# Layer 2's attention units in four steps instead of eight, and the places of three other groups of stages

## The chip, the core and the metric

The kernel runs on one core of a Trainium2 chip. The metric is the device time of one execution in microseconds. Before the change it is 1865.47 us, the median of three runs (1865.31 to 1870.87). One more execution was taken with the hardware profiler on: 1867.64 us, with a span of 1865.7 us from its first to its last instruction.

## What is computed

Four decoder-like layers run one after the other on x, 16 x 64 rows of 512 numbers. Each layer adds an attention over a context of the same shape and then a feed-forward part ("ffn"), and a layer norm stands before each of the eight. The code counts from zero (l0, f0, l1, f1 ...); this text says layer 1 for l0 and f0, layer 2 for l1 and f1, layer 3 for l2 and f2.

```python
x = x + L0_xattn(layernorm(x), ctx)   # layer 1: 8 heads, window of 16
x = x + L0_ffn(layernorm(x))          # int8-like quantised silu gate
x = x + L1_xattn(layernorm(x), ctx)   # layer 2: 32 query heads of 128, 8 key heads, RMS norm on q and k
x = x + L1_ffn(layernorm(x))          # one 512x512 product of MXFP4-quantised x and weight
x = x + L2_xattn(layernorm(x), ctx)   # layer 3: 32 heads of 16, 8 key heads
x = x + L2_ffn(layernorm(x))          # top 16 of 64 experts of rank 16
x = x + L3_xattn(layernorm(x), ctx)
x = x + L3_ffn(layernorm(x))
```

In layer 2's attention q and k of each head are divided by their root mean square, the scores go through a softmax, and the weighed values of four query heads go through a slice of the output matrix that is added to x. Its products are made three times (high times high, high times low, low times high part), for precision.

## The kernel before, in words

x lies in SBUF as eight tiles of 128 rows (NT = 8, two sequences each). The work is cut into stages, named by layer and part, and each stage has an index. A stage is a function on each of the engines that take part in it (TensorE, VectorE, ScalarE, GpSimd, SyncE for loads). `stage_order()` writes one list of (stage, index), ORDER, and every engine runs its own part of each stage in exactly that order; what crosses engines is held by semaphores. So the list sets each engine's queue. An instruction that waits holds everything behind it on its engine.

The list is made by pipelines. `pipeline(starts, stages, first)` gives, step by step, stage k of the unit that started k steps ago, latest stage first, but the stages named in `first` ahead of all. `beside(main, side, at)` makes one step of a main pipeline with two steps of a side pipeline: one ahead of it and one behind its first `at` stages.

- Layer 1's attention has 32 units (tile, quarter) of eight stages, one a step, 39 steps. Its ffn tiles are the side, one tile every eight side steps, that is every four main steps, with 13 stages (the last three make the layer norm and the transpose of layer 2). `at` is 4: in a step the order is side, l0_sum, l0_out, l0_weigh, l0_turn, side, l0_scores, l0_project, l0_rows, l0_norm.
- Layer 2's attention has 64 units (key head h, tile t; i = 8h + t) of eight stages: l1_a (12 query matmuls of 512 columns into bank 0 and 24 key and value matmuls of 256 into bank 1), l1_n (VectorE scales q and k by the reciprocal root mean square, which ScalarE's squares and GpSimd's power make), l1_b (transposes), l1_s (scores, row maximum, exps), l1_z (reciprocal, GpSimd's product), l1_t (probabilities turned), l1_v (weighing), l1_d (12 output matmuls and the addition to x). The order in a step is n, d, v, t, z, s, b, a. For the last head the copies of l1_b are ScalarE's, otherwise VectorE's.
- At the last tile of a head, ScalarE and VectorE split the next head's weights into high and low parts (`high_parts`, `low_parts`). At units 20, 24, 28 and 32 l1_d first quantises a tile of the ffn's weight (`mxfp4`, 11 VectorE instructions).
- The ffn tiles of layer 2 start with the last eight units. Each has eight stages: f1_stats, f1_norm, f1_quant (mxfp4), f1_turn, f1_mm, then l2_stats, l2_rows, l2_turn. f1_turn, f1_mm and l2_turn all use PSUM bank 3, which l1_b's keys also use.
- Behind the 71 steps `l2_begin` makes layer 3's keys and values in four groups of 12 matmuls, all four in bank 3. Then layer 3's attention starts (l2_q, l2_a, l2_s, l2_z, l2_t ...).

PSUM has eight banks. `psum_uses` gives each stage's banks; where a stage has several, they are taken in turn. A use waits until the last one of its bank is freed. In layer 1 the pair (6, 7) serves l0_out, the queries and keys of l0_project, and all the stages of the ffn with l1_turn.

Lines of the profile that the text speaks of: L557 a transpose of integers (f0_turn, f0_turn2), L564 a bf16 transpose (f1_turn), L608 layer 1's scores, L645 l0_out, L606 the band in front of the scores, L591 l0_project, L688 and L700 the queries and keys of l1_a, L712 l1_b, L724 l1_s, L732 l1_t, L739 l1_v, L749 l1_d; on VectorE L1157 the addition of l0_out, L1185 the silu's reciprocal, L1193 its end, L1047 a layer norm's rows, L1229 l1_n, L1086 the first of mxfp4, L1026 a layer norm's statistics; on GpSimd L1907 the power, L1882 the silu's product, L1849 the masked queries of l0_project; on ScalarE L1607 the keys' copy in l1_b.

Of the kernel before, what the change touches and what calls it, by code (L numbers as in the profile page):

```python
# [9 lines left out]
BF16 = mybir.dt.bfloat16  # L10
# [7 lines left out]
NT = 8  # L18
# [42 lines left out]
def stage_order():  # L61
    order = []
# [13 lines left out]
    def beside(main, side, at):  # L76

        run(1, side)
        got = next(main, [])
        order.extend(got[:at])  # L80
        run(1, side)
        order.extend(got[at:])
# [8 lines left out]
    l0 = ["l0_norm", "l0_rows", "l0_project", "l0_scores", "l0_sum", "l0_turn", "l0_weigh", "l0_out"]  # L91
# [34 lines left out]
    order.append(("f2_begin", 0))  # L126
    run(16 + 6 - 4, pipe2)
# [5 lines left out]
    for _ in range(10):  # L133
        beside(att3, ffn3, 3)
# [10 lines left out]
def psum_uses(stage, i):  # L145
# [15 lines left out]
    if stage in ("f0_gate", "f0_turn2", "f0_down", "l1_turn"):  # L161
        return [("p", (6, 7))]
    if stage == "l1_a":
        return [("q", (0,)), ("k", (1,))]
# [8 lines left out]
    if stage == "l2_begin":  # L173
        return [(k, (3,)) for k in range(4)]
# [108 lines left out]
def build_program(nc, d, out):  # L283
    ctx = ExitStack()
    with ctx:
# [137 lines left out]
        al = carve(R0, RF)  # L423
        CPt, CP = slots(al, 2, 528), slots(al, 3, 512)
# [4 lines left out]
        wq0, wk0, wv0 = al(128), al(128), al(128)  # L429
        wo0 = al(8 * 128).rearrange("p (h n) -> p h n", h=8)  # L430
        wob = CXf[0][:, 64:192]
        bq0, bk0, bo0 = al(1), al(1), al(1)
        bv0, hm = al(1), al(8)
        pad, band, bandb = al(384), al(640), al(640, BF16)
# [96 lines left out]
        def lt_user(kind, t):  # L531

            return {"l1": None, "l2": ("l1_a", 56 + t, "k"), "f2": ("l2_q", t // 2, 3), "l3": ("f2_h", t, 1),
                    "f3": ("l3_q", 24 + t // 4 * 4, 3)}[kind]


        def tensor_program(pe):
# [141 lines left out]
            def l1_a(i):  # L679
# [1546 lines left out]
```

## Time and profile before

| | |
|---|---|
| median of three runs | 1865.47 us |
| profiled execution | 1867.64 us, span 1865.7 us |
| TensorE matmuls busy | 1717.2 us, 92% |
| VectorE, ScalarE, GpSimd busy | 871.2, 712.5, 515.7 us |
| mean granted TensorE clock | 0.959 |
| DMA | 54.01 MB, mean 29 GB/s |

The granted clock is a share of full speed: 1 is 2.4 GHz, 0.5 is 1.2 GHz, and a stretch's value is the mean over both. The page cuts the span into 40 slices; each digit is the busy share of one in tenths:

```profile
PE   7999999689999999999999965699999998999997
PEclk9999889899999999999999987799999999999999
```

A row of the timeline gives start, duration, engine, line, operation, what it writes and reads and how many were merged; in brackets the idle time of the engine just before it and who ended it. Matmuls overlap, so the time that one takes from its engine is the distance to the next start, and not its duration.

### The profile page before, as it was taken

The numbers are of one execution on the slowest core, as the hardware profiler recorded it, in microseconds if no ns is written. First come the engines' busy times: TensorE is split into PE (matmuls) and PEld (weight loads), VectorE is DVE, ScalarE is ACT, GpSimd is POOL, SyncE is SP. The second block draws the span as 40 slices with busy tenths as digits, with TensorE's granted clock in tenths as the row PEclk, the third lists the DMA queues.
The fourth block names the chain that finished last, engine by engine and source line by source line (L and its number), as shares of the span: only waits on it lengthen the run. The fifth ranks groups of instructions, "written<-read, shape, count | busy, mean of one in ns | idle before, by whom it ended". The sixth has DMA issues, their size and how long they took to land. (4 is left out here: it accounts for less than half of the span.)

```text
span 1865.7 us, 26016 instructions
## 1 busy us (share of the span) xinstructions
PE 1717.2 (92%) x9694; PEld 1390.1 (75%) x9698; DVE 871.2 (47%) x1772; ACT 712.5 (38%) x2384; POOL 515.7 (28%) x615
## 2 busy tenths in 40 slices
PE   7999999689999999999999965699999998999997
PEld 5877787578888888888888853466555676777775
DVE  3566566444343445443433356567653321243344
ACT  3443333335454544444545531133221112354441
POOL 5566554222222221222222222233210000421122
PEclk9999889899999999999999987799999999999999
DMA  7000000111010000010101000020000012010000
GB/s 213 13 6 7 7 1 1 57 51 35 5 53 24 35 24 35 22 36 1 57 18 40 7 1 1 23 93 35 1 1 18 1 40 71 18 40 23 1 12 34
DMA packets 25709, 54.01 MB, mean 29 GB/s; under 512 B 14944, under 2 KB 16352, under 8 KB 22128
## 3 DMA queue, kind: packets, MB, share of 16 engines
q1 hardware_dynamic: 24048, 51.85, 8.3%
q8 instruction: 77, 1.26, 0.3%
q10 hardware_dynamic: 1472, 0.51, 0.1%
q14 instruction: 48, 0.39, 0.1%
q0 software_dynamic: 64, 0.00, 0.0%
HBM read 50.25 MB, written 2.10 MB: 28 GB/s over the span
## 5 line engine op out<-in xcount | busy, mean ns | idle before, releaser
L1912 POOL TENSOR_TENSOR big<-big 128x512 f32<-128x512 f32 x96 | 101.1, 1053 | 417.4 <-DVE big L1262 416.5
L1229 DVE TENSOR_TENSOR big<-pb,big 128x512 f32<-128x512 f32 x64 | 44.2, 691 | 362.3 <-POOL big L1907 362.3
L1617 ACT ACTIVATE big<-pb,big 128x128 f32<-128x128 f32 x384 | 135.7, 366 | 186.9 <-issue 113.7
L749 PE MATMUL pb<-woh,oh 128*128 128x512 f32 (+1 forms) x384 | 157.6, 411 | 2.5 <-DVE ol L1268 0.5
L1051 DVE TENSOR_TENSOR X<-X,pb 128x512 f32<-128x512 f32 x128 | 87.2, 681 | 148.1 <-PE pb L749 87.7
L1586 ACT ACTIVATE big<-pb 128x128 f32<-128x128 f32 x384 | 106.7, 278 | 123.6 <-PE pb L688 58.3
L749 PE MATMUL pb<-wol,oh 128*128 128x512 f32 (+1 forms) x384 | 153.5, 400 | 0.0
L749 PE MATMUL pb<-woh,ol 128*128 128x512 f32 (+1 forms) x384 | 153.1, 399 | 0.0
L700 PE MATMUL pb<-wkl,CXh 128*128 128x256 f32 x512 | 144.3, 282 | 0.0
L700 PE MATMUL pb<-wkh,CXh 128*128 128x256 f32 x512 | 144.1, 282 | 0.0
L700 PE MATMUL pb<-wkh,CXl 128*128 128x256 f32 x512 | 143.9, 281 | 0.0
L1633 ACT CAST oh<-pb 128x512 fp32r<-128x512 f32 (+1 forms) x96 | 56.0, 584 | 200.2 <-PE pb L739 199.9
L688 PE MATMUL pb<-wqh,CXh 128*128 128x512 f32 x256 | 110.0, 430 | 23.9 <-DVE big L1229 22.9
L1902 POOL TENSOR_SCALAR big<-big 128x6 f32<-128x6 f32 x64 | 12.8, 199 | 371.9 <-ACT big L1586 371.9
L688 PE MATMUL pb<-wqh,CXl 128*128 128x512 f32 x256 | 104.3, 407 | 0.0
L688 PE MATMUL pb<-wql,CXh 128*128 128x512 f32 x256 | 104.1, 407 | 0.0
L739 PE MATMUL pb<-big 128*128 128x256 f32 (+1 forms) x384 | 99.4, 381 | 0.0
L700 PEld LDWEIGHTS pb<-wkh,CXh 128*128 128x128 f32 x512 | 96.9, 189 | 3.0
L700 PEld LDWEIGHTS pb<-wkl,CXh 128*128 128x128 f32 x512 | 96.7, 189 | 3.0
L700 PEld LDWEIGHTS pb<-wkh,CXl 128*128 128x128 f32 x512 | 97.0, 190 | 0.0
L749 PEld LDWEIGHTS pb<-woh,oh 128*128 128x128 f32 (+1 forms) x384 | 74.7, 194 | 19.5 <-DVE ol L1268 6.1
L1907 POOL TENSOR_TENSOR big<-big,half 128x6 f32<-128x6 f32 x64 | 84.8, 1324 | 9.4
(246 smaller groups left out, 4066.8 us busy)
## 6 DMA issues: line engine op xcount, KB each, us to landing
big<-in_w SPq DMA_DIRECT2D x21, 1024.0 KB, 5.0
big<-in_w SPq DMA_DIRECT2D x8, 512.0 KB, 5.4
big<-in_w SPq DMA_DIRECT2D x4, 768.0 KB, 4.2
X<-in_x SPq DMA_DIRECT2D x8, 256.0 KB, 6.0
big<-in_cn SPq DMA_DIRECT2D x8, 256.0 KB, 2.7
CXlf<-in_cT SPq DMA_DIRECT2D x8, 256.0 KB, 5.3
big<-in_wa SPq DMA_DIRECT2D x1, 2048.0 KB, 7.6
big<-in_wb SPq DMA_DIRECT2D x1, 2048.0 KB, 12.0
```

Of the source, the lines that this page charges most:

```text
L688: a = pe.matmul(bank(p), x_rows(x, c, t), y[:, 512 * c:512 * c + 512], start=(n == 0), stop=(n == 11))
L700: a = pe.matmul(bank(p)[:, s * 256:s * 256 + 256], kv_rows(x, c, 2 * t + s), y[:, 256 * c:256 * c + 256], start=(n == 0), stop=(n == 11), ...
L739: a = pe.matmul(bank(p)[0:hd, s * 256:s * 256 + 256], v_of(s), pt[:, s * 256:s * 256 + 256], start=(s == 0), stop=True, skip_group_check=True)
L749: a = pe.matmul(bank(p), x[0:hd, 512 * k + h * 128:512 * k + h * 128 + 128], y[0:hd, 512 * h:512 * h + 512], start=(n == 0), stop=(n == 11))
L1051: v.tensor_tensor(X[:, t, :], X[:, t, :], bank(p), ADD).then_inc(p.free, 1)
L1229: v.tensor_tensor(quarters(qn[i % 2]), quarters(bank(p)), bc(rr[i % 2][:, 0:4], 128), MUL).then_inc(p.free, 1)
L1586: y = a.activation(sq[i % 2], src, ACT.Square, accum_out=ss[i % 2][:, j:j + 1])
L1617: y = a.activation(e_[:, c], bank(p)[:, c], ACT.Exp, bias=m[j % 2][:, k:k + 1], scale=1.0, accum_out=z[j % 2][:, k:k + 1])
L1633: a.copy(high[0:hd, k:k + 512].rearrange("p (h b q) -> p b h q", h=4, b=2), bank(p)[0:hd].rearrange("p (b h q) -> p b h q", b=2, h=4)).the ...
L1902: g.tensor_scalar(ss[i % 2][:, 0:6], ss[i % 2][:, 0:6], 1.0 / 128, 1e-6, MUL, ADD).then_inc(*on.to(S.pool))
L1907: g.tensor_tensor(rr[i % 2][:, 0:6], ss[i % 2][:, 0:6], half[:, 0:6], ALU.pow).then_inc(*on.to(S.rr))
L1912: g.tensor_tensor(quarters(e_), quarters(e_), bc(r[j % 2], 128), MUL).then_inc(*on.to(S.pn))
```

## The change

`beside` goes. `together(stages, *sides)` puts side steps at chosen places between the stages of one step, and `unit_steps` gives the stages of a step from a list with a delay for each, in the order in which the list has them.

- Layer 1: the same delays and nearly the same order, but the two side steps stand at places 2 and 5: l0_sum, l0_out, side, l0_weigh, l0_turn, l0_scores, side, l0_project, l0_rows, l0_norm. l1_turn uses bank 3 (with l0_turn) instead of the pair (6, 7). `l1_begin` stands three steps earlier; ScalarE waits there for layer 1's last scores and no longer for its last output, and buffers are laid out so that the two don't overlap.
- Layer 2: l1_a becomes l1_q and l1_k. The delays are 0 for q, k, n; 1 for b, s, z; 2 for t, v; 3 for d. The order in a step is q, b, t, k, s, n, z, v, d. 67 steps instead of 71. ScalarE squares q and then splits the next query weights, squares k, copies v and then splits the key weights; VectorE's low parts of the key weights come behind l1_n. The first output weights are split at unit 2 (was 1), and mxfp4 stands behind the addition.
- The ffn of layer 2 has its side steps at places 3 and 6 of the steps 60 to 65, both behind the output in step 66, and the last eight in layer 3's first steps.
- Layer 3's keys: the four groups of `l2_begin` become the stage `l2_kv`, in banks 0 and 1 in turn; two in step 64 (where q and k have no unit any more) and two in step 65.

```diff
-    att0 = pipeline(range(4 * NT), [(s, every) for s in l0], ("l0_sum",))
+    l0 = [("l0_sum", 4), ("l0_out", 7), ("l0_weigh", 6), ("l0_turn", 5), ("l0_scores", 3), ("l0_project", 2),
+          ("l0_rows", 1), ("l0_norm", 0)]
-    l1 = ["l1_a", "l1_n", "l1_b", "l1_s", "l1_z", "l1_t", "l1_v", "l1_d"]
+    l1 = [("l1_q", 0), ("l1_b", 1), ("l1_t", 2), ("l1_k", 0), ("l1_s", 1), ("l1_n", 0), ("l1_z", 1), ("l1_v", 2),
+          ("l1_d", 3)]
-    att1 = pipeline(range(8 * NT), [(s, every) for s in l1], ("l1_n",))
-    ffn1 = pipeline([2 * t + 1 for t in range(NT)], [(s, every) for s in f1])
+    ffn1 = pipeline([2 * t for t in range(NT)], [(s, every) for s in f1])
+    l2_kv = pipeline(range(4), [("l2_kv", every)])
...
-    for _ in range(4 * NT + 7):
-        beside(att0, ffn0, 4)
-    order.append(("l1_begin", 0))
-    for _ in range(6):
-        beside(att1, ffn0, 4)
-    order.append(("f1_begin", 0))
-    run(7 * NT + 7 - 6, att1)
-    for _ in range(8):
-        beside(att1, ffn1, 4)
+    for step, stages in enumerate(unit_steps(4 * NT, l0)):
+        if step == 4 * NT + 3:
+            order.append(("l1_begin", 0))
+        together(stages, (ffn0, 2), (ffn0, 5))
+    for step, stages in enumerate(unit_steps(8 * NT, l1)):
+        if step == 6:
+            order.append(("f1_begin", 0))
+        if step < 6:
+            together(stages, (ffn0, 3), (ffn0, 6))
+        elif step < 60:
+            together(stages)
+        elif step < 64:
+            together(stages, (ffn1, 3), (ffn1, 6))
+        elif step == 64:
+            together(stages, (l2_kv, 0), (ffn1, 3), (l2_kv, 3), (ffn1, 6))
+        elif step == 65:
+            together(stages, (l2_kv, 0), (ffn1, 3), (ffn1, 6), (l2_kv, 9))
+        else:
+            together(stages, (ffn1, 9), (ffn1, 9))
     order.append(("l2_begin", 0))
+    run(1, pipe2)
     for _ in range(4):
-        beside(pipe2, ffn1, 3)
+        got = next(pipe2)
+        together(got, (ffn1, 0), (ffn1, min(3, len(got))))
...
-    if stage in ("f0_gate", "f0_turn2", "f0_down", "l1_turn"):
+    if stage in ("f0_gate", "f0_turn2", "f0_down"):
         return [("p", (6, 7))]
+    if stage == "l1_turn":
+        return [("p", (3,))]
...
-    if stage == "l2_begin":
-        return [(k, (3,)) for k in range(4)]
+    if stage == "l2_kv":
+        return [("p", (0, 1))]
...
             def l1_begin(_):
-                on.wait_ge(l0_done.free, l0_done.n + 1)
+                read = PSUM["l0_scores", 4 * NT - 1, "S"]
+                on.wait_ge(read.full, read.n + 1)
                 high_parts(wqh, wq1, 128, 4, D.wq1, 16, S.wqh)
                 high_parts(wkh, w1, 128, 2, D.kv1, 16, S.wkh)
```

## Rows read from the trace of the kernel before

**Rows 1.** Windows by stretch: length, then busy us of each engine, granted clock, DMA share, GB/s.

```profile
28.00:343.00 315.00, 293.19 (x2176) 248.90 (x2176) 196.08 (x384) 121.07 (x223) 166.16 (x191) 0.93 0.05 16
...
420.00:1043.00 623.00, 613.28 (x3796) 547.03 (x3795) 271.65 (x541) 309.06 (x1316) 138.90 (x163) 0.99 0.08 29
...
1082.00:1232.00 150.00, 91.01 (x381) 67.49 (x384) 85.89 (x182) 30.86 (x77) 38.56 (x52) 0.80 0.08 29
```

**Rows 2.** Timeline, a plain step of layer 2, TensorE and VectorE.

```profile
561.16 0.40 PE L749 MATMUL pb<-woh,oh 128*128 128x512 f32 x1
...
563.90 1.03 PE L739 MATMUL pb<-big 128*128 128x256 f32 x4
563.92 0.69 DVE L1229 TENSOR_TENSOR big<-pb,big 128x512 f32<-128x512 f32 x1 [7.16 <-POOL big L1907]
...
564.76 0.60 PE L732 MATMUL pb<-ident,big 128*128 128x128 f32 x4
...
565.20 1.06 PE L724 MATMUL pb<-big 128*128 128x128 f32 x8
...
566.10 0.82 PE L712 MATMUL pb<-ident,big 128*128 128x128 f32 x6
...
566.67 0.48 PE L688 MATMUL pb<-wqh,CXh 128*128 128x512 f32 x1
```

**Rows 3.** TensorE's waits, 420 to 1060: releaser, us in total, times, longest.

```profile
PE pb L688 <- DVE big L1229: 9.7, 9, 3.4
```

**Rows 4.** Timeline of TensorE behind a long wait of layer 2.

```profile
717.71 0.77 PE L688 MATMUL pb<-wqh,CXh 128*128 128x512 f32 x1 [3.40 <-DVE big L1229]
```

**Rows 5.** Timeline of VectorE, one quantisation in the hand-over (first, and the next behind it).

```profile
1087.16 0.68 DVE L1086 TENSOR_REDUCE big<-xn 128x16 f32<-128x512 f32 x1
...
1092.30 0.69 DVE L1026 BATCH_NORM_STATS2 st<-X 128x6 f32<-128x512 f32 x1
```

**Rows 6.** Timeline of TensorE, the ffn's turn behind it.

```profile
1096.43 0.59 PE L564 MATMUL pb<-identb,big 128*128 128x128 bf16 x4 [8.61 <-ACT big L1607]
```

**Rows 7.** TensorE's waits, 1082 to 1233.

```profile
PE pb L564 <- DVE big L1110: 17.2, 4, 4.4
```

**Rows 8.** TensorE's waits, 40 to 320.

```profile
PE pb L557 <- DVE X L1157: 12.6, 6, 2.5
```

**Rows 9.** Timeline of TensorE in layer 1, a period of four steps.

```profile
202.35 1.94 PE L557 MATMUL pb<-ident,big 128*128 128x128 f32 x8 [2.23 <-DVE X L1157]
...
204.76 3.67 PE L608 MATMUL pb<-big 128*128 128x64 f32 x16
...
214.64 1.95 PE L645 MATMUL pb<-big 128*128 128x128 f32 x16
...
218.20 0.38 PE L606 MATMUL pb<-big 16*128 16x512 bf16 x1
...
220.35 1.11 PE L591 MATMUL pb<-big 128*128 128x128 f32 x8
...
221.52 1.95 PE L645 MATMUL pb<-big 128*128 128x128 f32 x16
...
246.13 1.69 PE L557 MATMUL pb<-ident,big 128*128 128x128 f32 x8 [2.23 <-DVE X L1157]
```

**Rows 10.** Timeline of VectorE in the same period.

```profile
217.92 1.75 DVE L1185 RECIPROCAL big<-big 128x256 f32<-128x256 f32 x1
...
222.23 1.79 DVE L1047 TENSOR_SCALAR xn<-X,mv,rs 128x512 f32<-128x512 f32 x1
...
234.05 0.54 DVE L1047 TENSOR_SCALAR big<-X,mv,rs 128x512 bf16<-128x512 f32 x1
```

**Rows 11.** Timeline of GpSimd in the same period.

```profile
221.00 0.67 POOL L1882 TENSOR_TENSOR big<-big 128x256 f32<-128x256 bf16 x1 [3.27 <-DVE big L1193]
221.81 1.93 POOL L1849 TENSOR_TENSOR big<-big 128x1024 f32<-128x1024 f32 x1
```

**Rows 12.** TensorE's waits, 343 to 420.

```profile
PE pb L688 <- DVE big L1229: 13.2, 5, 6.8
```

More of the change, by code:

```diff
@@ L74, in run, with together, unit_steps @@
             n += 1
[L76 to L82, printed above, removed]
+    def together(stages, *sides):
+        for k in range(len(stages) + 1):
+            for side, at in sides:
+                if at == k:
+                    run(1, side)
+            if k < len(stages) and stages[k] is not None:
+                order.append(stages[k])
+    def unit_steps(n, stages):
+        for step in range(n + max(late for _, late in stages)):
+            yield [(name, step - late) if 0 <= step - late < n else None for name, late in stages]
     def odd(u):
@@ L133, in stage_order @@
     for _ in range(10):
-        beside(att3, ffn3, 3)
+        got = next(att3, [])
+        together(got, (ffn3, 0), (ffn3, min(3, len(got))))
     order.append(("end", 0))
@@ L691, in l1_a, with l1_k @@
                 a.then_inc(p.full, 1)
[L692 removed]
+            def l1_k(i):
+                h, t = divmod(i, NT)
+                p = PSUM["l1_k", i, "p"]
                 on.wait_ge(S.ctl, 8)
@@ L783, in f1_mm, with l2_kv @@
                 a.then_inc(p.full, 1)
-            def l2_begin(_):
+            def l2_kv(k):
+                hf, which = divmod(k, 2)
+                p = PSUM["l2_kv", k, "p"]
                 on.wait_ge(S.w2l, 2)
-                for k in range(4):
-                    hf, which = divmod(k, 2)
-                    p = PSUM["l2_begin", 0, k]
-                    on.wait_ge(p.free, p.n)
-                    n = 0
-                    for c in range(4):
-                        for x, y in three(CXh, CXl, w2h, w2l):
-                            a = pe.matmul(bank(p), y[:, 256 * c + which * 128:256 * c + which * 128 + 128],
-                                          ctx_rows(x, c, hf),
-                                          start=(n == 0), stop=(n == 11))
-                            n += 1
-                    a.then_inc(p.full, 1)
+                on.wait_ge(p.free, p.n)
+                n = 0
+                for c in range(4):
+                    for x, y in three(CXh, CXl, w2h, w2l):
+                        a = pe.matmul(bank(p), y[:, 256 * c + which * 128:256 * c + which * 128 + 128],
+                                      ctx_rows(x, c, hf),
+                                      start=(n == 0), stop=(n == 11))
+                        n += 1
+                a.then_inc(p.full, 1)
             def l2_q(n):
@@ L1282, in l1_d @@
                 n = weight_quant(i)
+                add_x(t, PSUM["l1_d", i, "p"])
+                if t == NT - 1 and h < 7:
+                    low_parts(wol, woh, wo1[h + 1], 128, 4, S.woh, S.wol, h + 1)
                 if n is not None:
@@ L1663, in f1_turn, with l2_kv @@
                 copy_bf16(PSUM["f1_turn", t, "p"], quarters(xT4[t % 2]))
[L1665 to L1678 removed]
+            def l2_kv(k):
+                hf, which = divmod(k, 2)
+                p, read = PSUM["l2_kv", k, "p"], PSUM["l1_k", 8 * NT - 1, "p"]
+                on.wait_ge(read.full, read.n + 1)
+                on.wait_ge(p.full, p.n + 1)
+                if which == 0:
+                    y = a.copy(K2[:, hf * 512:hf * 512 + 512], bank(p))
+                else:
+                    for s in range(2):
+                        y = a.copy(V2[:, hf * 1024:hf * 1024 + 1024]
+                                   .rearrange("p (b s k) -> p b s k", s=2, k=64)[:, :, s, :],
+                                   bank(p).rearrange("p (b k) -> p b k", b=8))
+                y.then_inc(p.free, 1)
             def l2_q(n):
```

125 lines of the change are left out of this document (58 added, 67 removed).

## The prediction

> **What bounds the kernel now.** I read the windows by stretch first, then TensorE's waits in each stretch, then the timeline around the longest. TensorE sets the time. In the middle of layer 2 (420 to 1043 us) it is busy 613.28 of 623 us at a granted clock of 0.99; in layer 1 (28 to 343) 293.19 of 315 at 0.93; in the hand-over from layer 2 to layer 3 (1082 to 1232) only 91.01 of 150 at 0.80, with VectorE at 85.89 [rows 1]. So what can move the time is TensorE's idle time, the half clock behind it, and a new wait in the 623 us where it is full.
>
> Letters: q, k, b, s, t, v, d are layer 2's stages of one unit (queries, keys and values, transposes, scores, turned probabilities, weighing, output).
>
> **Layer 2, the full stretch.** The matmuls are the same; their order changes. q(i+1) needs bank 0, which VectorE's l1_n(i) frees; that needs the squares of k(i) on ScalarE and GpSimd's power. Now d, v, t, s, b stand between k and the next q: 566.67 - 561.16 = 5.51 us. In the new order b and t stand ahead of k, and s (566.10 - 565.20 = 0.90), v (564.76 - 563.90 = 0.86) and d (563.90 - 561.16 = 2.74) are left: 4.50 us. l1_n is done at 563.92 + 0.69 = 564.61, 3.45 us after 561.16 [rows 2]. So the chain is covered with 1.05 us over, and I cost it at nothing. With the cover gone, each microsecond costs 57, once a unit. The row maximum of unit i-1 now comes ahead of l1_n(i) on VectorE, but is done 1.7 us after k (0.90 of scores and a pass like L1229's 0.69), before the power is. The other pairs of stages have q or k (12 and 24 matmuls) between their two sides.
> TensorE's waits for l1_n here are 9.7 us in 9, the longest 3.4 [rows 3], and two of them have that length. Those come where a head ends (weights split on ScalarE ahead of the squares) and a weight tile is quantised on VectorE in front of the addition. Behind the one at 717.71 the clock is half: a 512-column matmul takes 0.77 there, and 0.48 at 566.67 [rows 2, 4]. I estimate 1.6 and 3.4 us lost so: 14.7 us in all. In the new order the squares of q go first and the quantisation stands behind the addition. It takes 1092.30 - 1087.16 = 5.14 us [rows 5]; behind the addition it makes the copies of the next b late by 0.45 us in a plain step and about 1.75 where a head ends, twice each: 4.4 us. Term: **-10 us**, bounds -13 and 0.
>
> **The hand-over, layer 2 to 3.** d(i) is now in step i+3, not i+7, so the first ffn tile enters at step 60, while q and k still run. A full step has 70 matmul records (12 q, 24 k, 6 b, 4 t, 8 s, 4 v, 12 d); 3796 of them in 613.28 busy us [rows 1] make 11.3, and I use 11.2. Now, from the start of q(60) at about 1043 to layer 3's first turned probabilities at 1232, 189 us pass. At q(60) the old order owes TensorE three d, three v, one s (2.74, 0.86, 0.90) and two t (0.44, 565.20 - 564.76) [rows 2] more than the new one: 12.6 us that will lie earlier. Like for like 176.4 us.
> The new order step by step: step 60 takes 11.2. Step 61: a turn more, 11.5. Step 62: the ffn's matmul waits about 1.65 us for bank 3 (key copies on ScalarE behind the squares) and the next turn 2.4 for the quantisation: 16.3. In step 63 the turn waits for bank 3, which a ScalarE copy frees that is queued behind the exps; they wait for a row maximum that is behind the quantisation. The row at 1096.43 shows this pattern: quantised by 1092.30, turned at 1096.43, a wait of 8.61 [rows 5, 6]. I take 3.6 us behind the quantisation, with one copy in place of two: a wait of 5.4, step 19.7. Step 64, with two groups of layer 3's keys (2.8 each) in the place of q and k: 18.6. Step 65: 16.7. Step 66 and the turn behind it: 10.4. That is 104.4; layer 3's q(0), s(0), s(1), q(1) (two times 7.8, two times 1.9) with the last ffn tiles between them take 31: 135.5 us, so 41 less. Against it: five waits of 2.4 to 5.4 us with half clock behind them, some 9 us. Term: **-32 us**, bounds -41 (no half clock) and -18 (three steps keep waits of 8 us as at 1096.43). The quantisation itself was already a wait of 17.2 us in 4 [rows 7] and stays.
>
> **Layer 1.** Its ffn tiles come every four steps. The wait at 202.35 is 2.23 us for VectorE's addition of the output (L1157), queued behind the ffn's quantisation; six make 12.6 us [rows 8]. It is followed by half clock: the scores' 16 matmuls take 3.67 us at 204.76, where 218.20 to 220.35 has them and the band's in 2.15. A period is 246.13 - 202.35 = 43.8 us [rows 9]; over four I count 43.0. The ffn's stages behind the addition, and bank 3 for l1_turn, take this wait away.
> What is late next: the second ffn slot now stands behind the scores. In the silu's step VectorE first does the scores' maximum and subtraction (1.5 us, two passes), then the silu (3.3 us, 1.75 of it the reciprocal), then GpSimd multiplies (0.81 to the next start), and only then makes the masked queries (1.93) [rows 10, 11]: about 7.6 us after the scores end. TensorE has the projection (221.52 - 220.35 = 1.17) and output, weighing and turn (218.20 - 214.64 = 3.56) before the next scores need them: 4.7 [rows 9]. A new wait of 2.9 us per tile. In the same step the key projection waits 1.45 us for a ScalarE copy that now stands behind the exp. With two smaller ones (1.05 and 0.45) that is 5.9 us of waits on some 36.3 of work: 42.2 at full clock. A wait of 2.23 us was followed by half clock, so 2.9 will be, at 2 to 3.5 us: period 44.6, 1.6 more than 43.0, five times: **+8 us**. Bounds -5 (no half clock) and +16 (twice the half clock).
> A tensor_scalar of VectorE takes 1.79 us at 222.23, beside GpSimd's masked queries at 221.81, and 0.54 at 234.05 [rows 10, 11]. The sum has 1.2 for it.
> The Trainium skill, "GPSIMD Engine Reference", section 1 (Specifications), says that GpSimd shares its SBUF interfaces with VectorE and that they contend when VectorE runs a two-port mode or has two SBUF inputs. By that rule the ffn's rows, moved beside the masked-query product, take 1.79 each, which adds some 3 us in five periods; by the short row alone it would be 3 us less. The trace's two rows agree with the rule.
>
> **Layer 1 to 2.** The first weights are split three steps earlier, so q(0) follows the last output. Now TensorE waits 13.2 us in 5 for l1_n from 343 to 420, the longest 6.8 [rows 12], about 19 with the others, and some 8 us by the clock. In the new order I find 4.1, 0.8, 3.4, 2.2 and small ones (the first output weights are split in step 2 ahead of l1_n), 13 in all, and 7 by the clock. Term: **-7 us**, bounds -15 and +3 (the splits hold up ScalarE in layer 1's last steps by 3.5 us).
>
> **Sum.** -10 - 32 + 8 - 7 = -41 us. The profiled execution took 1867.6 us (span 1865.7, the rest lies around it); the median of the runs is 1865.5, 2.1 lower. So 1867.6 - 41 = 1826.6, less 2.1: **1825 us** (rounded up by half).
>
> **Rivals.**
> (a) Layer 1's waits go and no new one comes: 43.0 falls to about 38 a period, -25 us in place of +8. For it: the wait for L1157 is the only long one there. Against: the chain from silu to masked queries. 1825 - 33 = 1792.
> (b) The hand-over gives half of its term back, and layer 1 takes its upper bound. For it: VectorE is one queue there with 5.14 us per tile, and ScalarE's copies stay behind the exps. 1825 + 16 + 8 = 1849.
> (c) Slower: the loop bank 0, l1_n, q. If l1_n comes later than now by more than the 1.05 us left over, every full step waits; from 0.7 us a step (l1_n 1.8 us late) the 41 us are gone, and at 1.2 us the time is 1825 + 68 = 1893. For it: the squares, the row maximum and the exps now follow k closely on two engines. Against: ScalarE has nothing left to do when k ends, and the row maximum is over before the power.
> (d) The stages stand in the step list as the change says, so "it does something else" gets no chance.
>
> **How the numbers follow.** Forecast 0.60, (a) 0.14, (b) 0.17, (c) 0.09. The likeliest one's own range is 1805 to 1845. The range 1792 to 1855 takes in (a) and (b) and leaves (c) out. A measurement of this kernel tells 0.3% (5.6 us) from no change. Faster: all but (c) and a tail of (b), 0.87. Within: 0.05. Slower: most of (c), 0.08.
>
> **What would show it.** Right: no wait for l1_n in a plain step between 440 and 680, against one at every q in (c). In layer 1 every four steps a wait of the scores for GpSimd's masked queries of about 3 us, none for L1157, and half clock as often as now. In the hand-over TensorE's waits for the quantisation and for ScalarE's copies of 2 to 5 us, about 25 us in sum and not 59. Wrong: from q(60) to layer 3's first turned probabilities over 160 us or under 130, or a period of layer 1 under 41 us.

## The result and the profile after

The changed kernel takes 1874.3 us (median of 16 runs, 1869.01 to 1878.5), the kernel before 1865.65 (16 runs, 1862.54 to 1870.87). The ratio is 1.0041, 95% interval 1.0031 to 1.0052: 0.4% slower, clear of noise though small, where 1825 us, 2.2% faster, was forecast. The profiled execution has a span of 1872.6 us, 6.9 more than before. Of all executions below one is left out, of e14, which took 4387 us.

I cut both spans at four instructions that both kernels have: the first addition of l0_out, the first query matmul of layer 2, the 61st l1_n, and layer 3's first turned probabilities. "Half clock" is the time in a stretch for which the record of the granted clock says 0.5.

| stretch | before | after | difference | forecast | half clock before, after |
|---|---|---|---|---|---|
| start to first l0_out | 40.7 | 39.0 | -1.7 | 0 | 3.4, 0 |
| layer 1, to the first q | 301.8 | 349.0 | **+47.2** | +8 | 41.0, 95.6 |
| layer 2, to the 61st l1_n | 708.6 | 704.0 | -4.6 | -4.4 | 30.7, 10.2 |
| hand-over to layer 3 | 181.1 | 143.2 | -37.9 | -44.6 | 61.4, 34.1 |
| rest | 633.4 | 637.5 | +4.0 | 0 | 14.9, 20.5 |

The forecasts are the prediction's terms on these cuts: the 12.6 us of work that lies earlier is added in layer 2 and taken off the hand-over. So layer 1 alone turned 40 us of gain into 7 of loss; the other stretches came within 7 us of their forecasts. The start is when the first data come; it lies at 38.8 to 42.3 us in all the profiles below, without a pattern, so I compare kernels by the stretches.

The windows of the kernel after, for [rows 1] (length, busy us of each engine, granted clock, DMA share, GB/s):

```profile
28.00:388.00 360.00, 310.07 (x2168) 260.53 (x2167) 200.40 (x384) 120.13 (x222) 167.85 (x188) 0.87 0.04 12
465.00:1082.00 617.00, 614.06 (x3822) 547.04 (x3821) 291.05 (x547) 309.86 (x1335) 141.13 (x165) 1.00 0.09 30
1082.00:1235.00 153.00, 113.09 (x561) 88.64 (x560) 93.40 (x197) 45.31 (x148) 42.38 (x61) 0.89 0.02 8
```

In layer 1 TensorE is busy 310.07 us with 2168 matmul records where it was 293.19 with 2176: 17 us more for the same work, at a clock of 0.87 and not 0.93. And it is idle 49.9 of 360 us, not 21.8 of 315: 28 us more. Both kinds of loss are there, and idle time is the larger one: 28 of the 45 us between the two windows.

TensorE's waits from 40 to 345 us, which leaves out the end of this layer 1 (releaser, total, times, longest), for [rows 8]:

```profile
PE pb L632 <- POOL big L1886: 22.8, 10, 3.2
PE pb L583 <- DVE big L1090: 6.9, 4, 2.5
PE pb L671 <- ACT big L1573: 4.3, 5, 1.7
PE pb L611 <- ACT big L1573: 3.2, 5, 0.8
```

L632 is the band ahead of the scores, L1886 GpSimd's masked queries, L583 the ffn's turns, L1090 VectorE's quantisation, L611 the key projection, L671 l0_out, L1573 a copy of the ffn's turned integers. No wait for the output's addition is left. The timeline of one period, TensorE, for [rows 9]:

```profile
206.59 0.39 PE L632 MATMUL pb<-big 16*128 16x512 bf16 x1 [3.23 <-POOL big L1886]
206.91 3.24 PE L634 MATMUL pb<-big 128*128 128x64 f32 x16
212.85 2.04 PE L611 MATMUL pb<-big 128*128 128x512 f32 x2 [0.56 <-ACT big L1573]
222.82 2.00 PE L634 MATMUL pb<-big 128*128 128x64 f32 x16
230.55 0.38 PE L632 MATMUL pb<-big 16*128 16x512 bf16 x1 [1.32 <-POOL big L1886]
230.86 3.30 PE L634 MATMUL pb<-big 128*128 128x64 f32 x16
238.87 2.02 PE L671 MATMUL pb<-big 128*128 128x128 f32 x16 [0.49 <-ACT big L1573]
```

VectorE and GpSimd ahead of the first wait, for [rows 10, 11]:

```profile
199.56 0.69 DVE L1170 TENSOR_TENSOR big<-pb,big 128x512 f32<-128x512 f32 x1
200.49 1.75 DVE L1213 RECIPROCAL big<-big 128x256 f32<-128x256 f32 x1
203.19 0.29 DVE L1221 TENSOR_SCALAR big<-big 128x256 bf16<-128x256 f32 x1
```

```profile
203.57 0.90 POOL L1919 TENSOR_TENSOR big<-big 128x256 f32<-128x256 bf16 x1 [9.73 <-DVE big L1221]
204.62 1.92 POOL L1886 TENSOR_TENSOR big<-big 128x1024 f32<-128x1024 f32 x1
```

This is the chain that the prediction named: subtraction, silu, product, masked queries, scores; the wait was forecast at 2.9 us and is 3.23. The wait of 1.32 us is for masked queries too; there GpSimd starts them at 228.33, behind the power for l1_stats, a stage of the ffn tile's side step, for which it had waited on VectorE's statistics. But the scores' 16 matmuls take 3.24 us behind it and 2.00 at 222.82, and a wait of only 1.32 us at 230.55 is followed by 3.30. The clock record has two stretches of half clock in this period, 10.2 us from 207.4 and 6.8 from 231.3; a period before had one, 10.2 us from 202.1.

The prediction reckons with 36.3 us of TensorE's work in a period at full clock. The mean of five periods, from the eighth l0_out to the 28th, splits so (us; the loss at half clock is the busy time over 36.3):

| | period | TensorE idle | lost at half clock | half clock in five |
|---|---|---|---|---|
| before | 42.6 | 2.7 | 3.6 | 41.0 |
| forecast | 44.6 | 5.9 | 2.4 | |
| after | 50.0 | 7.1 | 6.7 | 78.5 |

TensorE's waits from 1060 to 1240, for [rows 7]:

```profile
PE pb L590 <- ACT CXhf L1496: 19.1, 4, 7.6
PE pb L590 <- DVE big L1138: 11.1, 3, 4.4
PE pb L811 <- ACT big L1645: 3.4, 3, 1.5
```

From q(60) to layer 3's first turned probabilities TensorE is idle 39.9 us; before it was 59.0, and about 25 were forecast.

### The profile page after: what moved, and what is told of

Same layout as the page of the kernel before. It is cut to its first block and busy times, and to the rows that moved or that the text cites. A ratio compares the mean times of both kernels' runs of the same rounds, so it can differ in the third digit from the quotient of the medians.

```text
span 1872.6 us, 25970 instructions
## 1 busy us (share of the span) xinstructions
PE 1726.9 (92%) x9698; PEld 1395.6 (75%) x9698; DVE 892.2 (48%) x1772; ACT 706.1 (38%) x2384; POOL 517.4 (28%) x615
## 5 line engine op out<-in xcount | busy, mean ns | idle before, releaser
L778 PE MATMUL pb<-woh,oh 128*128 128x512 f32 (+1 forms) x384 | 165.6, 431 | 4.2 <-ACT big L1573 1.7
L778 PE MATMUL pb<-woh,ol 128*128 128x512 f32 (+1 forms) x384 | 151.9, 396 | 0.0
L1286 DVE TENSOR_REDUCE big<-pb 128x4 f32<-128x512 f32 x96 | 66.1, 688 | 179.4 <-PE pb L753 164.9
L729 PE MATMUL pb<-wkh,CXh 128*128 128x256 f32 x512 | 150.3, 294 | 0.0
L714 PE MATMUL pb<-wqh,CXh 128*128 128x512 f32 x256 | 103.3, 404 | 10.3 <-DVE big L1256 10.3
L768 PE MATMUL pb<-big 128*128 128x256 f32 (+1 forms) x384 | 103.3, 393 | 0.0
L1844 POOL TENSOR_SCALAR ve<-mv 128x1 f32<-128x1 f32 x64 | 15.7, 245 | 283.1 <-DVE mv L1058 280.4
L1276 DVE COPY big<-pb 128x512 f32<-128x512 f32 x56 | 38.7, 691 | 109.2 <-PE pb L741 108.8
```

Source lines behind the costliest of these rows:

```text
L714: a = pe.matmul(bank(p), x_rows(x, c, t), y[:, 512 * c:512 * c + 512], start=(n == 0), stop=(n == 11))
L729: a = pe.matmul(bank(p)[:, s * 256:s * 256 + 256], kv_rows(x, c, 2 * t + s), y[:, 256 * c:256 * c + 256], start=(n == 0), stop=(n == 11), ...
L768: a = pe.matmul(bank(p)[0:hd, s * 256:s * 256 + 256], v_of(s), pt[:, s * 256:s * 256 + 256], start=(s == 0), stop=True, skip_group_check=True)
L778: a = pe.matmul(bank(p), x[0:hd, 512 * k + h * 128:512 * k + h * 128 + 128], y[0:hd, 512 * h:512 * h + 512], start=(n == 0), stop=(n == 11))
L1276: v.tensor_copy(QT[i % 2].rearrange("p (b h q) -> p h b q", b=2, h=4), bank(p).rearrange("p (h b q) -> p h b q", h=4, b=2)).then_inc(p.fre ...
L1286: v.tensor_reduce(m[j % 2], quarters(bank(p)), AX, MAX, negate=True).then_inc(S.m, 1)
```

## The experiments

"Layer 1" is the stretch from the first l0_out to the first q; a period is the mean of the five from the eighth l0_out to the 28th. The last column counts whole each record of half clock that starts between 28 us and the first q; so it is up to 9 us more than what lies in layer 1 (44.4 here for the kernel before, 41.0 above). Stretches come from one profiled execution, times are medians of 4 to 9. The ratio is to the kernel before as executed in the same session, where its median was 1865.4 (e1 to e8), 1869.9 (e9 to e12) and 1865.6 us (e13 to e16).

| kernel | us | ratio, 95% interval | layer 1 | period | half clock to first q |
|---|---|---|---|---|---|
| before | 1865.6 | | 301.8 | 42.6 | 44.4 |
| after | 1874.3 | 1.0041 [1.0031, 1.0052] | 349.0 | 50.0 | 95.6 |
| e1 after, layer 1 as before | 1840.7 | 0.9855 [0.9836, 0.9874] | 303.1 | 42.8 | 47.8 |
| e2 after, 2nd side at 4 | 1861.2 | 0.9976 [0.9964, 0.9988] | 334.8 | 47.5 | 78.5 |
| e3 after, 16-row filler | 1869.0 | 1.0023 [1.0007, 1.0040] | 339.7 | 48.8 | 64.9 |
| e4 after, split late | 1877.4 | 1.0057 [1.0041, 1.0074] | 348.3 | 50.3 | 99.0 |
| e5 before, layer 1's edits | 1917.4 | 1.0274 [1.0247, 1.0302] | 344.2 | 49.5 | 85.3 |
| e6 e1, l1_turn in bank 3 | 1809.7 | 0.9697 [0.9673, 0.9721] | 282.2 | 38.8 | 13.7 |
| e7 e6, l0_out first | 1807.4 | 0.9681 [0.9659, 0.9702] | 280.5 | 38.6 | 17.1 |
| e8 e7, four l2_turns in bank 2 | 1796.3 | 0.9627 [0.9604, 0.9649] | 279.0 | 38.3 | 13.7 |
| e9 after, 2nd side at 6 | 1858.3 | 0.9936 [0.9917, 0.9955] | 330.9 | 47.1 | 58.0 |
| e10 e1, 16-row filler | 1833.0 | 0.9814 [0.9794, 0.9834] | 305.5 | 42.9 | 54.6 |
| e11 e8, split early | 1797.9 | 0.9617 [0.9603, 0.9631] | 284.1 | 39.3 | 17.1 |
| e12 e1, keys as before | 1841.9 | 0.9859 [0.9843, 0.9875] | 301.7 | 42.6 | 44.4 |
| e13 e1, 128-row filler | 1821.2 | 0.9749 [0.9733, 0.9765] | 285.1 | 38.8 | 6.8 |
| e14 after, 128-row filler | 1863.9 | 0.9994 [0.9980, 1.0007] | 334.4 | 48.0 | 37.5 |
| e15 e6, 16-row filler | 1836.8 | 0.9835 [0.9818, 0.9852] | 311.8 | 44.5 | 54.6 |
| e16 e6, 128-row filler | 1815.6 | 0.9719 [0.9699, 0.9739] | 287.4 | 39.6 | 6.8 |

### Which part of the change costs: e1, e5, e4

e1 undoes layer 1's edits alone; e5 makes two of them alone in the kernel before; e4 puts only the split of the weights back.

```diff
-        if step == 4 * NT + 3:
-            order.append(("l1_begin", 0))
-        together(stages, (ffn0, 2), (ffn0, 5))
+        together(stages, (ffn0, 0), (ffn0, 4))
+    order.append(("l1_begin", 0))
...
     if stage == "l1_turn":
-        return [("p", (3,))]
+        return [("p", (6, 7))]
```

> The changed kernel with layer 1 as before: side steps at places 0 and 4, l1_turn in banks 6 and 7, the first weights of layer 2 split behind the last output. Theory A (the loss is all in layer 1: 45 us later at the first query matmul, in waits of the scores for GpSimd's masked queries, the half clock behind them and the early weight split): the first query matmul stands at about 343 us again, and the time is 1874 - 45 = 1829 us (1822 to 1836), 0.98 of the kernel before. Rival B (layer 2's new order or the hand-over gives some of it back elsewhere, or the loss in layer 1 is disturbed runs): the time stays over 1850.

> The kernel before with only two things of the change: layer 1's side steps behind the output's addition and behind the scores, and l1_turn in bank 3. Theory A (these two alone make layer 1 slow): periods of 47 to 53 us where it has 43, the first query matmul 33 to 40 us later, the time 1865 + 37 = 1902 (1893 to 1910). Rival F (the loss needs the new layer 2 order or the early split beside it): under 1880.

> The changed kernel with the first weights of layer 2 split behind the last output (l1_begin at the end of layer 1's steps) instead of three steps earlier. Theory A: output 28 no longer comes 13.9 us behind output 27 but about 7, and 3 us come back at the first query matmul, which waits for the split: the time is 1874 - 4 = 1870 (1865 to 1875). Rival E (the early split saves what it was meant to save): the time is 1875 to 1880.

With layer 1 as before, the rest is worth 25 us (1840.7, outside the 1822 to 1836 expected). The places and bank 3 in the kernel before lengthen its layer 1 by 42.4 us and its time by 52, so the loss does not hang on layer 2's new order. e5 went beyond the 1893 to 1910 us expected; in its profile 4.0 us more lie between the first q and the 61st l1_n and 2.5 in the hand-over. Putting the split back (e4) changes layer 1 by 0.7 us, so the early split is not the cause. It makes the kernel 3.1 us slower, not 4 faster: rival E was right, and the split three steps earlier saves a little. e1's distance to the 1829 us expected lies behind the first q: 712.6 us to the 61st l1_n, 704.0 after. The next experiment shows that this is l1_turn's pair of banks.

### The two edits of layer 1 apart: e6

```diff
     if stage == "l1_turn":
-        return [("p", (6, 7))]
+        return [("p", (3,))]
```

> The kernel of e1_l0_old (layer 1 as before, the rest as changed) with l1_turn in bank 3 as in the change. In e1 the first 60 units of layer 2 took 712.6 us from the first query matmul to the 61st normalisation, against 704.0 in the changed kernel and 705.6 with the split late. Theory G (l1_turn in banks 6 and 7 waits there for layer 2's weighing and output, which now start at steps 2 and 3): 704 to 706 again, so the time is 1840.7 - 7 = 1833 (1829 to 1837). Rival H (it is the side steps' place in layer 1 that leaves the ffn tile behind): 712 and 1840.

It brings 31 us, 20.9 of them in layer 1, where 4 to 12 in all were expected. So bank 3 for l1_turn was a gain with the old places. e4 and e6 differ in nothing but the side steps' places (2, 5 and 0, 4): 348.3 and 282.2 us of layer 1, 1877.4 and 1809.7 us in all. The places cost 66 us of layer 1. In the five periods e4 has 35.4 us of TensorE's idle time and e6 10.2; the same matmuls keep it busy for 216.0 and 183.8 us, with 81.9 and 6.8 at half clock. So of 57 us 25 are waits, and 32 the same matmuls taking longer. New places with l1_turn in the pair were not run, so each number holds only beside the other edit as it stood.

What the bank does: the same point of a period in e1 and in e6 (TensorE, idle time and releaser in brackets):

```profile
202.10 0.60 PE L572 MATMUL pb<-ident,xn 128*128 128x128 f32 x4
204.94 1.94 PE L582 MATMUL pb<-ident,big 128*128 128x128 f32 x8 [2.24 <-DVE X L1184]
206.81 0.60 PE L631 MATMUL pb<-big 16*128 16x512 bf16 x1
207.34 3.67 PE L633 MATMUL pb<-big 128*128 128x64 f32 x16
```

```profile
197.62 0.63 PE L572 MATMUL pb<-ident,xn 128*128 128x128 f32 x4 [1.21 <-ACT big L1551]
198.08 0.60 PE L582 MATMUL pb<-ident,big 128*128 128x128 f32 x4
199.07 0.63 PE L582 MATMUL pb<-ident,big 128*128 128x128 f32 x4 [0.39 <-DVE X L1184]
199.95 2.00 PE L633 MATMUL pb<-big 128*128 128x64 f32 x16
```

With the pair (6, 7), l1_turn takes the bank that has long been free, and leaves to the ffn's first turn the one with the newest output, whose addition it then waits for. In bank 3 l1_turn takes neither. One wait of 2.24 us becomes two of 1.21 and 0.39 with work between, and the scores behind them take 2.00 us and not 3.67. The rest of the gain is behind the first q: 703.9 us to the 61st l1_n, as after, and no longer 712.6.

### Moving the second side step: e2, e9

e2 has the places (2, 4), e9 (2, 6), after (2, 5).

> The changed kernel with layer 1's second side step ahead of the scores (place 4) and not behind them (place 5); all else as changed. Theory A (silu behind the scores on VectorE makes GpSimd's masked queries late, and that sets off everything): the wait for the masked queries falls from 26 us in 11 to under 5, a period of four steps from 48 to 52 us down to 40 to 43, the first query matmul comes at 345 to 355, the time is 1830 to 1842. Rival C (the side steps behind the output's addition are what costs, by late ffn stages on VectorE): periods stay over 46 and the time over 1860.

> The changed kernel with layer 1's second side step behind l0_project (place 6) instead of ahead of it (place 5). GpSimd makes the masked queries ahead of the silu's product, and TensorE makes the queries and keys ahead of the ffn's turns and matmuls; VectorE's queue keeps the score's maximum ahead of the silu. Theory A1 (the wait for the masked queries behind the silu's product, 25.8 us in 11, and the half clock behind it are most of layer 1's loss of 45 us): that wait is gone, a period falls from 49.5 us to about 43, time at half clock ahead of layer 2 from 95.6 to under 60, time 1874 - 25 = about 1849. Rival C (the second side place this far behind is too close to the next step's first side step, as place 4 was: two side stages follow each other with little of TensorE's work between, and the ffn's turn waits for VectorE): the wait moves to the ffn's turns and matmuls, 20 us or more of it, and the time stays at 1860 to 1875. Rival D (something else than waits): no change, 1874.

Both take the wait for the masked queries away, and both keep most of the loss. e2's longest waits in layer 1, then e9's:

```profile
PE pb L583 <- DVE big L1090: 26.9, 13, 5.4
PE pb L573 <- ACT big L1552: 9.0, 5, 2.1
```

```profile
PE pb L671 <- ACT big L1573: 17.8, 6, 3.0
PE pb L583 <- DVE big L1090: 9.4, 7, 2.1
PE pb L583 <- ACT big L1530: 9.2, 5, 2.5
```

These rows are 36 us in each, for other releasers than before. In the five periods TensorE is idle 29.2 us in e2 and 36.4 in e9; it was 35.4 in the changed kernel, 13.4 before and 10.2 in e6. Theory A and A1 forecast 1830 to 1842 and 1849 us; both failed, though the wait that they named went. Rival C came as it stands in e2 (period 47.5, 1861.2 us). In e9 it is the nearest. A1's half clock of under 60 us came (58.0), but not its period of 43 (47.1). The time is 1.7 us under C's range, and half of the waits are of l0_out for ScalarE's copy and not of the ffn's turns.

Why the places 0 and 4 wait so little is not shown. How evenly they cut TensorE's work in a step is not it. By [rows 9] l0_out, l0_weigh and l0_turn take 3.56 us together, the scores 2.15 and the projection 1.17; of the first the weighing is 217.61 - 216.52 = 1.09 and the turn 218.20 - 217.61 = 0.59:

```profile
216.52 1.16 PE L632 MATMUL pb<-big 64*128 64x128 f32 x16
217.61 0.66 PE L619 MATMUL pb<-ident,big 128*128 128x128 f32 x4
```

So places 0 and 4 cut a step into 3.56 and 3.32 us, and 2 and 5 into 3.83 and 3.05, hardly less evenly, with periods of 38.8 and 50.3 us (e6, e4). Places 2 and 4 (1.68 and 5.20) and 2 and 6 (5.00 and 1.88) are uneven and both a little faster than 2 and 5. All three have the first side step behind the output, and no run has only that one back at 0.

### What the half clock follows: e3, e10, and e13 to e16

Each adds matmuls into the bank of the next scores, which then write over the result. e3 and e14 have them ahead of the wait for the masked queries, the others ahead of the ffn's first turn. The 16-row filler, and the 128-row one that replaces it:

```diff
+                    for _ in range(9):
+                        pe.matmul(bank(spare), bandb[0:16, 0:128], bandb[0:16, 128:640], start=True, stop=True,
+                                  skip_group_check=True)
```

```diff
+                    for h in range(5):
+                        pe.matmul(bank(spare)[:, 0:256].rearrange("p (h c) -> p h c", h=2), wo0[:, h, :], wo0[:, 0:2, :],
+                                  start=True, stop=True, skip_group_check=True)
```

> The changed kernel with extra matmuls of the band (16 rows, 512 columns, into the scores' own bank, overwritten by the scores) ahead of the wait for the masked queries: 9 in each fourth step where the wait is 3 us, 4 in the one where it is 1.3. They keep TensorE active through the wait and change nothing else. Theory A1 (of the 5 to 10 us that a period lost, more than half is half clock behind the waits): low-clock time between 100 and 388 us falls from 85 us to under 35, the period to 43 to 45, the time is 1874 - 25 = 1849 (1840 to 1858). Rival D (the waits themselves are the loss, the half clock lies in other waits): the period stays at 48 or more, the time at 1870 or more.

> The kernel of e1 (layer 1 as before the change, the rest changed; 1840.7 us) with nine matmuls of the band into the next scores' bank ahead of each ffn's first turn, where TensorE waits some 2.2 us for VectorE's addition; their sums are written over by the next scores. They add no information and about 2 us of TensorE's work in the place of its wait. Theory H (in layer 1 the half clock follows these waits of 2.2 us, and it is what costs, not the waits): time at half clock ahead of layer 2 falls from 47.8 us to under 20, a period from 43 to about 41, time 1841 - 14 = about 1827. Rival R1 (the waits themselves cost, the half clock comes from elsewhere): half clock stays near 48, time 1841 or up to 5 us more, since the added work ends a little behind what it covered. Rival R2 (both, as in e3, where half clock fell by 31 us and the time by 5 only, since the fillers themselves ran over): 1836 to 1841 with half clock down by half.

> The kernel of e10 (1833.0 us; half clock 54.6 us ahead of layer 2) whose filler is another: five matmuls of 128 rows and 256 columns in f32 (about 2.1 us) in the place of nine of 16 rows and 512 columns. They write into the next scores' bank and are written over. Theory H2 (the clock falls after 2.2 us in which TensorE idles or works on 16 rows only, and the half clock is what costs): half clock falls from 54.6 us to under 20 and the time by 16 us, to about 1817. Rival R3 (the clock falls there for another reason than the wait): half clock 45 to 60, time 1833.

> The kernel of e3 (the changed kernel with a filler ahead of the wait for the masked queries; 1869.0 us; half clock 64.9 us ahead of layer 2) with five and two matmuls of 128 rows and 256 columns in the place of nine and four of 16 rows. Theory H2: half clock from 64.9 to under 30 us, time 1869 - 16 = about 1853. Rival R3: half clock 60 to 70, time 1869.

> The kernel of e6 (1809.7 us; half clock 13.7 us ahead of layer 2; no wait over 1.3 us in layer 1's full steps) with nine 16-row matmuls ahead of the ffn's turn in six tiles, 2.1 us each: 12 us of added work of TensorE, of which up to 1.3 us each lie in a wait. Theory H2 (for the clock they are as good as idle): the half clock comes back, 13.7 to 50 us or more, time 1810 + 10 + 18 = about 1838. Rival R3 (the clock follows something else): half clock stays near 14, time 1810 + 8 to 12 = about 1820.

> The kernel of e6 with five 128-row matmuls of 256 columns at the same place as in e15, the same 2.1 us each. Theory H2: half clock stays near 14 us, time 1810 + 8 to 12 = about 1820, some 18 us under e15. Rival R3: as e15.

e10 and e13, TensorE at the same point of layer 1:

```profile
200.41 2.11 PE L680 MATMUL pb<-big 16*128 16x512 bf16 x9
202.72 1.66 PE L582 MATMUL pb<-ident,big 128*128 128x128 f32 x8 [0.20 <-DVE X L1191]
204.31 0.60 PE L631 MATMUL pb<-big 16*128 16x512 bf16 x1
204.85 3.67 PE L633 MATMUL pb<-big 128*128 128x64 f32 x16
```

```profile
194.26 2.32 PE L680 MATMUL pb<-big 128*128 128x256 f32 x10
196.66 1.22 PE L582 MATMUL pb<-ident,big 128*128 128x128 f32 x8
197.81 0.39 PE L631 MATMUL pb<-big 16*128 16x512 bf16 x1
198.13 2.00 PE L633 MATMUL pb<-big 128*128 128x64 f32 x16
```

e3 and e10 came first, with 16 rows, and fitted no theory well. In e3 half clock fell from 95.6 to 64.9 us (under 35 expected by A1) and the time by 5.3 us (25 expected); the period of 48.8 is rival D's. In e10 the wait of 2.24 us is all but covered (0.20 left), half clock in layer 1 did not fall, and the time fell by 7.7 us. These two led to theory H2, and e13 to e16 test it.

e10's profile is of its slowest execution, 6.5 us above the median: its mean clock is 0.966 and that of the other three 0.971, which is some 19 us less half clock (twice what is missing to 1, times the span). So 54.6 is too much for a usual execution of e10, by an amount that is not known. In e13, e15 and e16 the profiled execution is within 2.3 us of the median.

Both fillers cover the wait. Behind 16-row matmuls the scores still take 3.67 us, behind 128-row ones 2.00. e13 is 19.5 us faster than e1 although TensorE has more to do. The other pair has the sharpest contrast: the same 2.1 us of filler in a kernel without that wait makes it 27 us slower (e15) or 6 (e16). In the five periods both are idle for the same 7.7 us; busy are 214.8 and 190.5 us, with 51.2 us at half clock and none. The windows from 28 us to the first q, e15, then e16:

```profile
28.00:351.00 323.00, 306.18 (x2222) 253.38 (x2221) 196.85 (x384) 121.69 (x223) 166.05 (x190) 0.92 0.05 16
```

```profile
28.00:330.00 302.00, 285.34 (x2231) 244.19 (x2231) 196.02 (x384) 121.38 (x223) 166.40 (x191) 0.99 0.06 17
```

The busy time is 94.8 and 94.5% of the two windows; only the clock differs, 0.92 and 0.99. Theory H2 (half clock is what costs, and it follows such a stretch) held in three. e13 came at 1821.2 (1817 expected), e15 at 1836.8 (1838), e16 21.2 us under e15 (18); R3 held in none. e14 is between: half clock falls to 37.5 us (under 30 expected), and the time by 5.1 us and not 16. Its period is still 48.0, for the waits are still there: 12.6 us for the ffn's quantisation, 8.5 for the masked queries, 7.6 for ScalarE's copies ahead of l0_out.

The two fillers differ in more than rows: 16 x 512 in bf16 against 128 x 256 in f32, from other tiles. Which of these counts for the clock was not separated; "16-row" and "128-row" are names here.

### Other parts, and a better version: e12, e7, e8, e11

e12 undoes the third part (layer 3's keys behind the last step, in bank 3). e7 puts l0_out ahead of l0_sum. e8 puts four of the l2_turns into bank 2:

```diff
+    if stage == "l2_turn" and i < 4:
+        return [("p", (2,))]
```

> The kernel of e1 (1840.7 us; layer 1 as before the change, the rest changed) with layer 3's keys and values made behind the last of layer 2's steps, four groups in bank 3, as before the change, and not in steps 64 and 65 in banks 0 and 1. It undoes the third part of the change alone. Theory M (the keys' place is a minor part of the hand-over's gain; each group of 12 matmuls, 2.8 us, covers a wait in steps 64 and 65, and in one bank each later group waits for the copy of the one before): the stretch from the 61st l1_n to layer 3's first turned probabilities goes from 143.9 to 151 to 156 us, time 1849 (1846 to 1853). Rival N (steps 64 and 65 are as long without the keys as with them, and behind the last step all of the 11.2 us and the copies' 4 us stand bare): 159 us, time 1856. Rival O (the ffn's chain of VectorE sets the hand-over's length and the keys are beside it wherever they are): 144 us, 1841.

> As e6_bank3, and in layer 1's steps l0_out stands ahead of l0_sum, so that VectorE adds the output 0.9 us earlier. Theory I (the wait of 2.23 us for that addition is what the half clock follows): the wait falls to about 1.3 us, the low-clock time in layer 1 from 48 us to under 15, a period from 43 to about 38, the time is 25 us under e6 (1800 to 1815). Rival J (the wait falls by 0.9 us and the half clock stays): 5 to 6 us under e6.

> As e7_out_first, and l2_turn of the first four tiles uses bank 2 and not bank 3, so that the ffn's turn behind it does not wait for a ScalarE copy that is queued behind the exps. Theory K (that copy is the 19.1 us in 4 of TensorE's waits in the hand-over, with 3.6 us of each behind the quantisation): from the 61st normalisation to layer 3's first turned probabilities 144 becomes 133 to 137, the time 7 to 11 us under e7. Rival L (VectorE's queue is the bound there, so the wait changes its name only): 0 to 3 us under e7.

> The kernel of e8 (1796.3 us) with the split of layer 2's first weights three steps earlier (step 35), as in the changed kernel. Theory E: the wait of 3.6 us of the first query matmuls for the weights' low parts goes, and half clock with it; the splits stand ahead of copies of layer 1's last steps and hold these up by less: time 1796 - 3 = 1793. Rival L: layer 1's last steps (27 to 34 wait more) lose as much as is gained, in the changed kernel out27 to out28 is 13.9 us where it was 6.4: 1796 or up to 1800.

The keys' place is worth 8.0 us of the hand-over (151.9 us against 144.0 in e1), as theory M says. The medians (1841.9, 1840.7) don't show it, where M expected 1849: in e12's profile the start is 3.1 us shorter, the rest 2.4 and layer 1 1.4, and the intervals of the two ratios overlap. So its worth for the whole kernel is not shown. e7 gains 2.3 us, within its interval; the wait of 2.24 us that it was to shorten had already gone with e6, so it tests neither of its theories. e8 takes 9.4 us off the hand-over (133.8 us, from 143.2), as theory K says, and, at 1796.3 us, beats both kernels: 3.7% under before, 4.2% under after. The early split (e11) takes the wait of 3.6 us for the weights' low parts away, and the stretch behind the first q is 2.4 us shorter; but the time is 1797.9, no gain. In its profile the five periods took 4.7 us longer than e8's, though the split stands behind them: so much one profile of layer 1 varies, and I read nothing smaller from the layer 1 column.

## Why the prediction was wrong, step by step

- **What bounds it, and layer 2.** Right. From the ninth l1_n to the 61st the time fell from 600.2 to 590.7 us, 9.5 less (forecast 10). From the first q to the ninth l1_n it is 4.9 us longer with 12.6 us of work moved in, so 7.7 less like for like (forecast -7). A plain step has no wait for l1_n, as the cover of 1.05 us said; rival (c) did not come.
- **Hand-over.** Mechanism right, 7 us short. Forecast waits of 1.65, 2.4 and 5.4 us are 1.48, 2.26 and 5.37 in the trace. At the last of layer 2's ffn tiles one of 7.60 stands (1221.01), which the sum did not have. From q(60) to layer 3's first turned probabilities 144.5 us were forecast and are 153.5: 39.9 of idle time where about 25 were expected, and 113.6 busy. So what was short is the waits, and not the 9 us for half clock.
- **Layer 1, the step that failed: "A wait of 2.23 us was followed by half clock, so 2.9 will be, at 2 to 3.5 us".** This term, 2.4 us a period, is mis-sized; 6.7 are lost at half clock. The waits were nearly right: the period from 204.74 to 254.28 has 3.23 + 0.56 + 1.32 + 0.49 = 5.6 us of them (forecast 5.9), the five periods 7.1 in the mean. The work was right: e6's periods of 38.8 us with 2.0 of waits leave 36.8, and 6.8 us of half clock lie in its five. So of the 5.4 us by which a period was missed some 4.3 are half clock, and the rest is waits. I took the half clock of one wait for the whole period. The smaller wait, forecast at 1.05 us and 1.32 at 230.55, was costed as a wait only; behind it stand 6.8 us of half clock, as behind some of 2.2 us before. "Half clock as often as now" was a sign of being right, and it came twice as often. The trace of before speaks against the term as well. A period of 43.0 with 36.3 of work, the wait of 2.23 [rows 9] and two more of 0.36 and 0.29 already lost 3.8 us at half clock, and I put 2.4 behind longer waits. Five periods of 7.4 more make 37 us, where 1.6 each had made 8. The ends of the layer, which I had not counted, make the other 10: 3 ahead of the eighth l0_out and 7 behind the 28th.
- **The path.** The costs of single waits were read well; what no term of the sum priced is that the new places as a whole are 66 us of layer 1 worse than the old ones (e4, e6). Why they are, beyond the waits listed, stays open.
- **A wrong alternative.** I priced rival (a), a period of 38 us, at 0.14 for this order. That period exists (e6, 38.8), but with the side steps at the old places and only l1_turn's bank changed. I had treated the two edits as one. The bank is -21 us of layer 1 (e1 to e6), and the places +66 beside it (e6 to e4).
- **Rivals.** (b) took layer 1's bound at +16, which was the upper end of my range; the true +47 is outside it. No rival was "layer 1 takes everything back".
- **The slow rows of VectorE.** The sum took a lengthened row of the ffn as 1.2 to 1.79 us. The trace after shows what sets the length:

```profile
228.33 2.16 POOL L1886 TENSOR_TENSOR big<-big 128x1024 f32<-128x1024 f32 x1
228.74 2.03 DVE L1090 TENSOR_SCALAR big<-big 128x512 f32<-128x512 f32 x1
232.93 1.93 POOL L1886 TENSOR_TENSOR big<-big 128x1024 f32<-128x1024 f32 x1
234.08 1.05 DVE L1088 TENSOR_SCALAR big<-big 128x512 f32<-128x512 f32 x1
235.17 0.43 DVE L1090 TENSOR_SCALAR big<-big 128x512 f32<-128x512 f32 x1
```

  GpSimd's first product ends at 230.49 and VectorE's row at 230.77, the second at 234.86 and 235.13; the pair of [rows 10, 11] at 223.74 and 224.02. Each row of VectorE ends 0.27 or 0.28 us behind a product that had started ahead of it, whenever it started itself. So 1.79 us is no fixed price: a row lasts until the product is done. The rule of shared SBUF interfaces ("GPSIMD Engine Reference", section 1, Specifications, of the Trainium skill) says that the two contend, and the trace agrees; which mode these rows run in no run here shows. The wait of 1.32 us is for the first of these products, which took 2.16 us where the median is 1.93; so 0.23 of it at most is such a clash.
- **The rest, which the prediction left at nothing.** Behind layer 3's first turned probabilities the changed kernel takes 4.0 us more. Of these 1.5 are idle time (27.8 against 26.3). In the kernels with the new layer 2 the rest follows its half clock: 634.9, 635.3, 636.0 and 637.4 us with 13.7, 14.7, 17.1 and 20.5. Before it was 633.4 with 14.9, some 2 us under that line; why is open, and so is what sets the half clock there.

## What to carry to other kernels

Price each new wait of TensorE twice: the wait, and the half clock that the trace shows behind waits like it; in this kernel 7.1 us of waits a period came with 6.7 more. Test such a price on the kernel before: its period has to come out of work, waits and half clock too. Cost the edits of one change one by one, above all a bank and a place, since here the small one was worth 21 us of layer 1 and the other lost 66. And don't expect one wait to be the loss: with the second side step moved ahead or behind, the named wait went and others took its place.

## What was not expected of the hardware

- A stretch of 2.1 us of 16-row bf16 matmuls was followed by half clock as a wait is: 54.6 us in layer 1 in e15, 6.8 in e16 with 128-row f32 matmuls of the same length at the same place. TensorE's busy share (94.8 and 94.5%) does not tell them apart.
- Adding work made the kernel faster: five 128-row matmuls per tile in a wait of 2.24 us are worth 19.5 us (e13 against e1).
- A tensor_scalar of VectorE on 128x512 in f32 took 2.03 us at 228.74 and 0.43 at 235.17, with the same form. In layer 1 of the traces before and after, 39 rows of a tensor_scalar from and to 128x512 in f32 take over 0.15 us more than the shortest of their line, and 37 of them end 0.28 us behind a GpSimd instruction that ran when they started.
